# Six more binned groups with a folded last block, in a one-core graph layer on Trainium2

## The reference, cut to what matters

```
h = relu(layernorm(x))
e = relu(concat([h[dst], edge_attr], 1) @ W1.T + b1)
e = relu(e @ W2.T + b2)
agg = segment_sum(e, src, 6250) / max(count(src), 1)
z = relu(concat([h, agg, u[0]], 1) @ Wa.T + ba)
out = x + z @ Wb.T + bb
```

## Time and profile before

| | |
|---|---|
| times of three runs | 1894.68, 1901.95, 1902.32 us, median 1901.95 us |
| the profiled execution | 1902.48 us, its span (first to last instruction) 1900.7 us |
| busy share of the span | PE 91%, POOL 79%, ACT 75%, DVE 71% |
| mean granted TensorE clock | 0.972 |
| DMA | 369 MB moved, 194 GB/s on average |

### The profile page before, as it was taken

One profiled execution on the slowest core, in us unless ns is written; L12 is line 12 of the kernel. 1 busy time (PEld: TensorE's weight loads), 2 busy tenths in 40 slices (PEclk: granted clock), 3 DMA queues, 4 the chain that ended last, 5 costly groups with the idle time before them and its releaser, 6 DMA issues.

```text
span 1900.7 us, 43131 instructions
## 1 busy us (share of the span) xinstructions
PE 1732.0 (91%) x12376; PEld 1463.0 (77%) x12376; DVE 1340.0 (71%) x4868; ACT 1428.0 (75%) x2591; POOL 1509.7 (79%) x991
## 2 busy tenths in 40 slices
PE   5898888999999999999899999999999999976828
PEld 3676777888888888888788888888888888866725
DVE  8665655777777777778677777777777777755727
ACT  4687877888888888888788888888888888842315
POOL 8488888888888888888888888888888888878850
PEclk9999999999999999999999999999999999988968
DMA  9988888999999999999899999999999999997755
GB/s 330 269 169 145 156 148 141 199 197 205 195 207 187 199 203 199 194 205 197 176 199 194 199 202 200 195 194 209 202 191 201 200 204 202 199 210 155 159 136 198
DMA packets 312201, 369.10 MB, mean 194 GB/s; under 512 B 40832, under 2 KB 196064, under 8 KB 311328
## 3 DMA queue, kind: packets, MB, share of 16 engines
q1 hardware_dynamic: 175200, 302.12, 55.1%
q0 software_dynamic: 135360, 62.15, 34.5%
q10 hardware_dynamic: 1408, 2.03, 0.3%
HBM read 203.87 MB, written 159.27 MB: 191 GB/s over the span
## 4 chain that ended last, share of the span: by engine, by line
POOL 53%; issue 20%; DMA 11%; PE 9%; ACT 3%; DVE 2%; SPq 1%; POOLq 0%; ACTq 0%; DVEq 0%
POOL sums L819 48%; DMA sums<-regA,idx 9%; POOL sums L807 5%; PE bank L1351 2%; PE bank L1400 2%; PE bank L1362 1%; DMA sums<-vscat,vidx 1%; PE bank L1374 1%; ACT h L921 1%; PE bank L1390 1%; ACT regA L929 1%; PE bank L1276 1%; PE bank L1476 1%; ACT regA L955 0%; DMA p_table<-regB 0%
## 5 line engine op out<-in xcount | busy, mean ns | idle before, releaser
L819 POOL DMA_INDIRECT sums<-regA,idx x844 | 1318.3, 1562 | 293.0 <-issue 242.6
L1351 PEld LDWEIGHTS bank<-h,regC 128*128 128x128 f32 x3072 | 387.4, 193 | 180.7 <-ACT h L940 127.8
L1351 PE MATMUL bank<-h,regC 128*128 128x130 f32 x3072 | 432.0, 284 | 64.5 <-ACT h L940 64.5
L1374 PE MATMUL bank<-regA,L 128*128 128x512 f32 x806 | 432.3, 619 | 2.8 <-DVE regA L1143 2.7
L1400 PE MATMUL bank<-w,h 128*128 128x128 f32 x3224 | 430.1, 277 | 0.0
L1400 PEld LDWEIGHTS bank<-w,h 128*128 128x128 f32 x3224 | 396.8, 194 | 1.1 <-ACT h L921 0.6
L921 ACT ACTIVATE h<-bank,b1c 128x512 f32<-128x512 f32 x403 | 275.6, 684 | 136.9 <-PE bank L1374 131.9
L1362 PE MATMUL bank<-regC 128*128 128x129 f32 x2352 | 296.9, 280 | 23.0 <-DVE regB L1130 12.7
L1390 PEld LDWEIGHTS bank<-h,regC 128*128 128x128 f32 x1688 | 218.9, 191 | 119.7 <-issue 91.3
L1362 PEld LDWEIGHTS bank<-regC 128*128 128x128 f32 x2352 | 277.4, 194 | 37.3 <-ACT vscat L961 21.9
L904 ACT ACTIVATE regC<-bank 128x520 f32<-128x520 f32 x384 | 231.8, 604 | 87.8 <-PE bank L1351 84.5
(11 more groups left out here) (143 smaller groups left out, 1526.9 us busy)
## 6 DMA issues: line engine op xcount, KB each, us to landing
regC<-slots SPq DMA_DIRECT2D x294, 260.0 KB, 5.6
regA<-in_ea SPq DMA_DIRECT2D x202, 256.0 KB
slots<-regC SPq DMA_DIRECT2D x192, 260.0 KB
src<-rows_src SPq DMA_DIRECT2D x107, 256.0 KB
slots<-regC SPq DMA_DIRECT2D x192, 138.1 KB
sums<-regA,idx POOLq DMA_INDIRECT x844
dstR<-rows_dst SPq DMA_DIRECT2D x101, 128.0 KB
sums<-zeros SPq DMA_DIRECT2D x20, 645.0 KB, 6.7
```

The costliest lines, as they stand in the source:

```text
L819: nc.gpsimd.indirect_dma_start(out=sums[k], out_offset=bass.IndirectOffsetOnAxis(ap=idx[:, n % RING, t:t + 1], axis=0), in_=scat[:, n % 4, ...
L1351: last = T.matmul(psSlot(t)[:, k, :], place, h2[:, g % 2, t, :], start=True, stop=True)
L1374: T.matmul(psL1(s % 2), L[:, s % RING, :], R[:, s % RING, :], start=True, stop=True).then_inc(l1_done, 1)
```

## The change

There are 198 binned groups, 3, 5, ..., 397, and 205 plain ones. The blocks are six of 32 and one of six. The block of six is *folded*: each of its four tiles goes to partitions of its own (6 x 16 = 96 partitions, one tile wide), so a unit of it needs two masks in place of eight and two products in place of eight, and its loads are two of 96 rows of 520 bytes. The last two blocks (`LATE`) have a schedule of their own: block 5 has one unit in every second step from 390 to 404, one a step from 405 to 409 and two a step to 415, and block 6 two a step from 416 to 428. Steps behind 402 hold no group. All units share three whole buffers, cut in quarters for the folded ones, in place of the six of the last block. From step 405 the products go to four banks of PSUM in turn, so that PE waits for the addition of three units earlier only.

SP issues the first loads of row numbers and attributes ahead of its wait for `p_table`. On DVE `rows_of(g)`, which writes `idx`, stands at the front of the step for the first groups. PE does three products of zeros behind the flag's sum, ahead of `mode_ready`. At the end the copies of `sums` wait for one array after another; `scat` lies behind the first half of `SA`, so these copies may start while other arrays are still added to. The count of digits covers 200 groups in place of 196.

```diff
-LAST_SORTED = 386
+FIRST_SORTED, LAST_SORTED = 3, 398
-BLOCK = 32
+SIZES = [32] * 6 + [6]
-ODD = 196
-NS = ODD * TPG
+NS = 200 * TPG
-ROUNDS = [[(0, 4), (4, 5)]] + [[(a, a + 4), (a + 4, a + 8)] for a in range(5, 45, 8)] + [[(45, 49)]]
+ROUNDS = [[(0, 4), (4, 5)]] + [[(a, a + 4), (a + 4, a + 8)] for a in range(5, 45, 8)] + [[(45, 49), (49, 50)]]
-UNIT_RING, SPARE = 3, 3
-TAIL_LAG, TAIL_LEAD = 5, 1
+UNIT_RING = 3
+LATE, LATE_LAG = 2, 5
+FOLD = [1] * 6 + [4]
...
+    steps = list(range(firsts[late], NG + 2, 2)) + list(range(NG + 2, NG + VSUM - 1))
+    steps += [NG + VSUM - 1 + n // 2 for n in range(LATE * UNITS - len(steps))]
...
+IDX_FIRST = 5
+APART = NG + 2
+ALONE = sum(len(units) for s, units in UNITS_AT.items() if s < APART)
...
-        o1 = RING * GE
+        o1 = max(RING * GE, 2 * NSETS * KC)
...
-            return bank[:, 0 if m >= PAIRED and m % 2 else 1, 0:PAIR * C]
+            return bank[:, 1 if m < ALONE else 2 + (m - ALONE) % 4, 0:PAIR * C]
...
+            load_ea(0)
+            sp.wait_ge(act_step, 1)
+            sp.wait_ge(rows_stored, 32)
+            load_dst_rows(0)
+            load_src_rows(0)
+            load_src_rows(1)
+            load_dst_rows(1)
+            load_ea(2)
...
-                    if buffer_of(m) >= UNIT_RING:
-                        sp.wait_ge(vpre_ready, NH)
-                    if len(users(m)) > 1:
-                        sp.wait_ge(unit_done, users(m)[-2] + 1)
+                    wait(sp, unit_done, UNIT_FREED[m])
+                    folded = slots.rearrange("n p (f x) -> n (p f) x", f=FOLD[k])
+                    rows = CAP * FOLD[k]
...
+                    for k in FIRST_OVER[0::2]:
+                        sp.wait_ge(added[k], 16 * SCATTERS[k])
+                        for b in range(2):
+                            r0, r1 = kept_rows(b, b + 1)
+                            sp.dma_start(SA[:, 0, k, b * KC:(b + 1) * KC], sums_v[k][:, r0 * C:r1 * C]).then_inc((acc_in[0], acc_second)[b], 16)
...
             for s in range(-3, STEPS + 1):
+                if is_plain(s - 3) and s <= IDX_FIRST:
+                    rows_of(s - 3)
...
-                        for t in range(TPG):
+                        for t in range(size):
                             made = VE.tensor_scalar(oh2[0:rows, m % 2, i, t, :], lows[0:rows, i, :], loaded(m)[0:rows, i, t, C:W], -float(b), ALU.subtract, ALU.is_equal)
...
+            pe.wait_ge(biasz_ready, 1)
+            for k in range(3):
+                T.matmul(psL1(1), ident[:, :], zeros[:, 0:GE], start=True, stop=True)
             pe.wait_ge(mode_ready, 1)
-            pe.wait_ge(biasz_ready, 1)
...
-                wait(pe, acc_ready, added_for(m))
+                wait(pe, acc_ready, m if m < ALONE else m - 3)
```

More of the change, by code:

```diff
@@ L91 @@
 NV = NH // 2
-BLOCKS = [BINNED[k:k + BLOCK] for k in range(0, NH, BLOCK)]
+BLOCKS = [BINNED[sum(SIZES[:k]):sum(SIZES[:k + 1])] for k in range(len(SIZES))]
+FOLD = [1] * 6 + [4]
 def src_row(g):
@@ L197, in build @@
+assert LO * NBIN == NKEPT >= N and OVER + PLACES == PW and 2 * OVER <= P and NH == 2 * NV and NG + max(VSUM, VLAG) < STEPS and NH == sum(SIZES)
+assert NBIN == BA * BA and PACK * BA <= P and NS == NPACK * PACK and PARTS[-1][1] == NPACK and (FIRST_SORTED - 1) * TPG + 2 * NS <= NT and all(len(units) == 1 for s, units in UNITS_AT.items() if s < APART)
 def build(nc, x, src_cols, dst_cols, src_rows, dst_rows, ea, u, w1t, b1, w2t, b2, wat, ba, wbt, bb, out):
```

158 lines of the change are left out of this document (83 added, 75 removed).

## The result

| | before | after |
|---|---|---|
| median of the runs | 1900.03 us (4 runs, 1894.68 to 1902.32) | 1912.15 us (4 runs, 1910.29 to 1914.98) |
| the profiled execution | 1902.48 us, span 1900.7 us | 1910.29 us, span 1907.7 us |

The ratio is 1.0072, with a 95% interval of 1.0055 to 1.0089: the changed kernel is slower by 0.7%. That is inside the range, but I had given no change 0.48 and slower 0.20. Lines are now those of the changed kernel: L846 and L834 are POOL's adds (plain and pair), L652 SP's unit loads, L1248 DVE's masks of a unit, L1396 PE's products of a unit, L1156 the addition into `acc`, L1162 and L1165 `idx`, L1487 `z_of_h`, L1503 the first transposes.

What follows compares the result with a forecast made beforehand. POOL's indirect adds bound the kernel until its last add, then the late units do. First chunk at 1843.8 us plus 54.5 us to the end gives 1898.3 us of span, with 1.8 us around it 1900 us; range 1884 to 1917 us.

Steps and rivals of the forecast that it cites:

- The bound and the mechanism: POOL's adds are the wall; units exposed behind the last groups spend the 42 us that POOL gains.
- POOL's end: POOL's last add: 1836.3 us less 39.6 us for 21 fewer adds and 2.8 us at the front, so 1793.9 us.
- The front: Start of the kernel: SP's earlier loads let POOL's fourth add start 2.8 us sooner, bounds 0 and 4.2 us.
- the three products of zeros: PE's added products in the front: counted at 0, bound 2.9 us.
- the zeros as the limit: POOL's fourth add, at 77.17 us before, waits for the last zero copy, which SP would issue sooner.
- DVE behind the last `idx`: Copy for group 402 begins 3.6 us behind group 398's last add; DVE is free for masks at 1767.1 us.
- Whole units: Behind the last groups: three at 2.2 us each, then 13 at 3.07 us, paced by loads into three buffers.
- The folded copies: Block 6's 49 loads, paced by SP's issue at 0.59 us each: 28.9 us, to 1839.5 us.
- a rival with 0.14: Folded loads cost SP 0.93 + 0.04 us each, 47.5 in place of 28.9 us: 1919 us; chance 0.14.
- The end: First chunk to the end: 3 us less than 57.5 us, with PE busy earlier and copies in: 54.5 us.
- rival (c): PE's clock falls to half among the whole units: 8.5 us, no gain at the end, 1911 us; chance 0.08.

Runs made afterwards that it cites:

- The kernel with six buffers: Changed kernel with e6's loads, `z_of_h` among the whole units, last `idx` five units later, fewer PE waits for `vscat` and six whole buffers: 1874.98 us, ratio 0.9868.
- e11: As e6, but with 49 folded copies, one a bin, each from 96 rows in a row: 1900.67 us, ratio 1.0009.
- e1: Changed kernel with one copy for a folded unit (25 in place of 49), last six groups' slots stored bin by bin: 1906.59 us, ratio 1.0048.
- e6: As e1, but the last six groups' slots lie place by place, so their stores are in rows again: 1893.98 us, ratio 0.9981.
- with three buffers: As the kernel with six buffers, but with the changed kernel's three whole buffers: 1884.92 us, ratio 0.9911.

## Why the prediction was wrong

The steps, as measured in the profiled execution:

| step | predicted | measured | off by |
|---|---|---|---|
| fourth add starts | 74.4 | 73.9 | -0.5 |
| POOL's last add ends | 1793.9 | 1790.4 | -3.5 |
| DVE free behind the last `idx` | 1767.1 | 1761.8 | -5.3 |
| first folded load issued | 1810.6 | 1809.0 | -1.6 |
| 49 folded copies | 28.9 | 36.5 | **+7.6** |
| first chunk | 1843.8 | 1850.2 | +6.4 |
| first chunk to the end | 54.5 | 57.5 | **+3.0** |
| span | 1898.3 | 1907.7 | +9.4 |

The rest of the way from 1900 to 1912 us lies outside the span: the profiled execution took 2.6 us around it where I had counted 1.8 us, and the median of the runs is 1.9 us above that execution. The forecast's own terms give 1767.1 + 6.6 + 39.9 = 1813.6 us for the end of (5,24), not the 1815 us that the later steps start from; this 1.4 us was in no term.

**The bound and the mechanism were right.** POOL was the wall before, its adds went away as counted, and the exposed units spent the gain. Leaving block 6's units out shows it directly (40 us), and the kernel with six buffers has POOL's end within 2 us of the changed one's and is 38 us faster.

**POOL's end** came 3.5 us earlier than worked out. From the fourth add on POOL took 1716.5 us for 916 adds, where 937 took 1759.1 us before: 42.6 us for 21 adds, 2.03 us each. But an average add, waits included, took 1.877 us before and 1.874 us after. So 39.4 us are the 21 adds, as in the sum, and 3.2 us are 916 adds that waited a little less, for which I had no row. In ten profiled kernels with this front and these adds (those with other stores or groups left out) POOL's end lies between 1790.1 and 1794.0 us, so these 3.2 us are no more than the scatter.

**The front** was right in the step that mattered, the fourth add. I priced the three products of zeros at nothing. They took 2.84 us, and layer 1 of the first two groups behind them 1.88 us in place of 3.75, at a granted clock of 1.00 in place of 0.50, so the clock gave 1.9 of the 2.8 us back; the DMA share of 45 to 50 us is full, and the fourth add is 3.3 us earlier than before. My reason for it, the zeros as the limit, holds only in the executions in which the first add comes early.

**DVE behind the last `idx`.** It was free 5.3 us earlier than worked out. POOL gives 3.5 of them. The rest is a row read wrongly: the 3.6 us from group 398's last add to the copy for 402 in the earlier trace rows end a wait for PE (L1390), not for the add. When PE was done early, the copy followed the add by 1.95 us:

```profile
1757.26 1.54 POOL L846 DMA_INDIRECT sums<-regA,idx  x1 [0.30 <-issue]
```

```profile
1760.75 0.60 ACT L956 ACTIVATE regA<-bank 128x520 f32<-128x520 f32 x1 [8.11 <-DMA sums<-regA,idx]
```

**Whole units**: the pace of 3.07 us was right. From (5,9) at 1762.06 to (5,24) at 1809.07 us it is 47.0/15 = 3.13 us. I was wrong in "By then (5,7) and (5,8) are done on PE", since only (5,7) was, and so in the 2.2 us for each of the first three. PE stood idle for 6.66 us for DVE's addition of (5,7), which stands behind the last `idx`; then it did (5,8) and (5,9) at the lower clock, 2.7 us each, and (5,10) was masked 5.4 us behind (5,9). This gave back 3.7 of the 5.3 us. That the first folded load was then issued within 1.6 us of the forecast is luck: two errors of opposite sign. PE's timeline there:

```profile
1762.29 0.77 PE L1458 MATMUL bank<-V,vS 128*128 128x129 f32 x2 [6.66 <-DVE regB L1156]
1763.43 5.46 PE L1396 MATMUL bank<-regC 128*128 128x129 f32 x32 [0.37 <-ACT vscat L988]
```

**The folded copies are the failed step**, a term of the sum that was sized too low. I wrote "I take 0.59 us, between the first two, since shape and source are nearest to them", and held 0.93 us for a rival with 0.14. They took 0.746 us apart. The choice of the nearest row went by bytes and source, and that was the wrong measure: e11 moved the same bytes from the same DRAM array at 0.50 us apart, with only the form of the source another (and, by the rule of the Trainium skill told with e1, the number of engines that follows from it). Nothing in rows 8 shows that form matters; but beside the 0.625 us for 260 KB of a whole unit they show copies of an eighth of that at 0.51 and 0.93 us, which should have told me that bytes are no guide. With a price half-way between the bounds, (0.51 + 0.93)/2 = 0.72, the sum would have been 1906.5 us.

**The end is the second.** "Now `z_of_h` runs right behind the last unit" left out the time that PE needs to get there. It was 6.1 us here, and 3.75 to 7.1 us in the other runs that have `z_of_h` there. How much of the 3.0 us it explains is less sure: the same kernel took 60.6 us from the first chunk to the end when it ran again, with a pause of 6.4 us. The trace of before shows it too, in PE's timeline behind its last unit, as two pauses that I had not read:

```profile
1812.93 0.67 PE L1453 MATMUL bank<-hT,wax 128*128 128x256 f32 x2 [2.63 <-issue]
1816.28 5.34 PE L1453 MATMUL bank<-hT,wax 128*128 128x256 f32 x14 [2.68 <-issue]
```

Under POOL's last 20 us these cost nothing. When the cover went, they came onto the path. The better clock that I had counted on did come (0.60 in place of 1.12 us for the first four transposes), and was just spent on that.

**The clock** (rival (c)): among the whole units it was 0.93, with two stretches of 3.4 us at the lower level. Among the folded ones it stayed at the lower level, while PE waited for SP. That did not set the pace, since SP did. Where the loads were faster (e6), the granted clock was 1.00 from 1811 to 1826 us; but with six buffers it fell to 0.50 at 1803 us although PE worked through 82 products without a pause that the profile shows. There PE at the lower level did set the pace (0.97 us a unit against DVE's 0.73 us), and in e11 it came level with SP's copies: what rival (c) describes, met among the folded units once their loads were fast enough. What decides the level there is open.

## What to carry to other kernels

Removing work from the bounding engine is worth only the cover that the rest can do without: count what stands behind the last release in program order, on every engine, not only on the one that you watch (here an addition that PE waits for, ACT's copy of `vscat` and PE's way out of the loop as well as DVE's masks). When DMAs run one behind another, price them by a row of the same form of addressing and not by their bytes, and lay the array out so that what is read last is read in one stretch and in few copies. A price that lies between rows a factor of 1.8 apart belongs in the middle of them, not at the near end.

## What the hardware showed that I had not expected

SP's time to issue a copy went by how it addresses its rows: 96 rows of 520 bytes took 0.69 us from six stretches of 16 rows and 0.43 us from one stretch of 96, and one copy of twice the bytes (96 rows of two pieces) no more, 0.45 us. In the changed kernel's main loop, the stores of 128 rows take 0.34 us, those of 68 rows 0.42 us, and the 60-row copy of `vpre`, the smallest of all, 0.93 us:

```profile
L634 SPq DMA_DIRECT2D slots<-regC x190: 292/424/518, 106.0 to 1699.0; - x190
```

```profile
L635 SPq DMA_DIRECT2D slots<-regC x190: 324/341/978, 106.5 to 1699.4; - x190
```

```profile
L639 SPq DMA_DIRECT2D V<-vpre x95: 914/930/1403, 103.2 to 1687.9; - x95
```

Two pairs were taken apart by an experiment. One is that of 96 rows. The other is the stores of the last six groups, the same bytes from the same rows of SBUF: 0.74 and 0.62 us into 17 and 32 bins, 0.37 and 0.34 us into 68 and 128 rows. The rest differ in more than their rows. That a dear form also lands late, and delays what stands behind it in the queue, is what the 13 us point to that POOL lost with the stores by bins; no landing of these stores was seen.

PE's pause of 4 to 7 us between its last step and the code behind the loop's branch stays open. Where `z_of_h` was moved ahead of it, the first transposes still came 1.3 us behind ACT's data in two kernels (1859.52 against 1856.91 + 1.28 us in the run with `z_of_h` among the whole units, and with three buffers) and at once in two others (with six buffers, 4.8 us behind the last unit), so it seems to lie at the place and not in `z_of_h`. Whether it is the jump over the other branch's instructions was not tried.
